# Attention and mixed FFN on one core: the order in which the on-chip tiles are allocated

## The chip, the cores and the metric

One Trainium2 chip, one of its cores. The metric is the device time of one execution in microseconds (us). The kernel before took 3089.31 us, the median of three runs (3080.82, 3089.31 and 3093.53).

## The reference, cut to what matters

```python
x = x + _layernorm(attn(_layernorm(x), w_qkv))      # x: 4 x 2048 tokens x 512
x = x + _layernorm(ffn(_layernorm(x), ...))

# attn: 16 heads of 32, windows of 128 tokens, each window sees the one before and the one after
scores = einsum('bhnqe,bhnke->bhnqk', q * scale, k_ctx)   # k_ctx: 3 windows, 384 keys
out = einsum('bhnqk,bhnke->bhnqe', softmax(scores), v_ctx)

# ffn, for each of the 4 sequences of 2048 tokens its own weights, 8 experts:
g = mean_s(relu(x @ gate_w1.T + gate_b1) @ gate_w2.T + gate_b2)   # 8 numbers per sequence
mW1 = W1 + sum_e g[e] * TW1[e];   mW2 = W2 + sum_e g[e] * TW2[e]   # biases likewise
out = gelu(x @ mW1.T + mb1) @ mW2.T + mb2                          # 2048 hidden units
```

All in float32.

## The kernel before, in words

The program is three functions that run one after the other, each with its own on-chip tiles, which are given back when it ends. In each, every engine has its own list of instructions, and semaphores order them.

`phase_qkv` (A) takes 16 chunks of 512 tokens: layernorm, transposition on TensorE (line 275), and the product with w_qkv (line 280). A float32 product is made as three products of float32r parts (high by high, high by low, low by high). A chunk has 8 groups of 12 matmuls for q and k (w is the stationary operand, the transposed x the moving one) and 4 groups of 12 for v (the other way round: x stationary, w moving). Results go to DRAM.

`phase_attention` (B) has 128 steps, each for two windows of four heads: scores (line 531, k moving) whose maximum VectorE takes (line 666), the transposed scores with the maximum as an added row (line 546, q moving), the exponential on ScalarE (line 637), sums on GpSimd (lines 491 and 501), and the products with v (line 573). The row of maxima is put into the q tile by two small DMAs of SyncE's queue (line 431).

`phase_gate_ffn` begins with the gate (C: residual, layernorm, transposition at line 1131, gate product at lines 1144 to 1146), and goes on to the FFN (E): VectorE mixes eight experts' weights into a base (line 1497) out of a ring that DMAs fill, ScalarE and VectorE split the result into high and low parts (slots 0 and 1 of five in the tiles wa, slots 2 to 4 in wb), and TensorE makes the hidden product (lines 1194 to 1196, weights stationary, y moving) and the output product (lines 1211 to 1213, u stationary, weights moving).

In the profile's rows the operands of a matmul stand as moving, stationary: `e_acc<-e_wa_hi,e_u_hi` has wa moving and u stationary.

What matters for this change is how a tile gets its address. The functions call `sb(name, shape, dtype)` once per tile:

```python
def sb(name, shape, dt):
    return ctx.enter_context(nc.sbuf_tensor("a_" + name, shape, dt))
```

Tiles are laid one behind the other in the order of these calls, in each of the 128 partitions at the same byte, each start rounded up to a multiple of 32 bytes. The first tile of each phase starts at byte 16512, which is a multiple of 128. The large tiles have sizes that are multiples of 1024 bytes, and so all that follow one another have the same offset within 128 bytes; the small ones (4 to 256 bytes) shift what comes behind them.

Of the kernel before, what the change touches and what calls it, by code (L numbers as in the profile page):

```python
# [8 lines left out]
F32 = mybir.dt.float32  # L9
F32R = mybir.dt.float32r  # L10

P = 128
D = 512
# [6 lines left out]
TILES = CH // P  # L20
CHUNKS = TOKENS // CH
EPS = 1e-5
QH = 4
# [4 lines left out]
RING = 9  # L28
# [15 lines left out]
def phase_qkv(nc, x, w_qkv, qk_dram, v_dram):  # L44
# [7 lines left out]
    with ExitStack() as ctx:  # L52
        def sb(name, shape, dt):
            return ctx.enter_context(nc.sbuf_tensor("a_" + name, shape, dt))
# [1 line left out]
        def sem(name):  # L56
            return nc.alloc_semaphore("a_" + name)

        eps = sb("eps", [P, 1], F32)
        stats = sb("stats", [P, TILES, 6], F32)  # L60
        moments = sb("moments", [P, TILES, 2], F32)
        std = sb("std", [P, TILES], F32)
        rstd = sb("rstd", [P, TILES], F32)
        w_in = sb("w_in", [P, KD, 3 * D], F32)
        w_hi = sb("w_hi", [P, KD, 3 * D], F32R)
        w_lo = sb("w_lo", [P, KD, 3 * D], F32R)
        x_in = sb("x_in", [P, 2, TILES, D], F32)
        xn = sb("xn", [P, 2, TILES, D], F32)
        xt_hi = sb("xt_hi", [P, 2, KD, CH], F32R)
        xt_lo = sb("xt_lo", [P, 2, KD, CH], F32R)  # L70
        qk = sb("qk", [P, SLOTS, 2, CH], F32R)
        v = sb("v", [P, 2, TILES, D], F32)
        ident = sb("ident", [P, P], F32)
        turn = [ctx.enter_context(nc.psum_tensor(f"a_turn{i}", [P, CH], F32)) for i in range(2)]
        acc = [ctx.enter_context(nc.psum_tensor(f"a_acc{i}", [P, CH], F32)) for i in range(BANKS)]

# [250 lines left out]
def phase_attention(nc, qk_dram, v_dram, o_dram):  # L327
# [7 lines left out]
    RING = 8  # L335
    BANKS = 3
    UNITS = 2 * QH
    with ExitStack() as ctx:
        def sb(name, shape, dt):
            return ctx.enter_context(nc.sbuf_tensor("b_" + name, shape, dt))  # L340
# [4 lines left out]
        def sem(name):  # L345
            return nc.alloc_semaphore("b_" + name)

        neg_max = sb("neg_max", [P, 2, 2, QH], F32)
        pick = sb("pick", [P, 2 * QH], F32)
        inv_sum = sb("inv_sum", [P, 2, 2 * QH], F32)  # L350
        q_st = sb("q_st", [P, QH, SEQ], F32R)
        k_st = sb("k_st", [P, QH, SEQ], F32R)
        v_sb = sb("v_sb", [P, W, QH * E], F32)
        ones = sb("ones", [P, 2, E], F32)
        probs = sb("probs", [P, RING, QH, 3 * WIN], F32)
        max_rows = sb("max_rows", [2 * QH, 2, WIN], F32R)
        total = sb("total", [P, 2, 2, QH, WIN], F32)
        ident = sb("ident", [P, P], F32)
        out_t = sb("out_t", [P, 2, 3, WIN], F32)
        out = sb("out", [P, 2, 2, QH * E], F32)  # L360
        ps_score = [psum(f"ps_score{i}", [P, 512]) for i in range(BANKS)]
# [392 lines left out]
def phase_gate_ffn(nc, x, gate_w1, gate_b1, gate_w2, gate_b2, o_dram, b1, b2, tb1, tb2, mix_rows,  # L754
# [12 lines left out]
    START = units[0][2]  # L767
# [38 lines left out]
    with ExitStack() as ctx:  # L806
# [3 lines left out]
        def sb(name, shape, dt, stack=ctx):  # L810
            return stack.enter_context(nc.sbuf_tensor("e_" + name, shape, dt))

        def psum(name, shape, stack=ctx):
            return stack.enter_context(nc.psum_tensor("e_" + name, shape, F32))

        w2g = sb("w2g", [P, KD, EXPERTS], F32)
        gate_bias = sb("gate_bias", [EXPERTS, 1], F32)
        gate_sum = sb("gate_sum", [P, KD, CHUNKS], F32)
# [8 lines left out]
        stats = sb("stats", [P, 2, TILES, 6], F32)  # L827
        moments = sb("moments", [P, 2, TILES, 2], F32)
        var = sb("var", [P, 2, TILES], F32)
        rstd = sb("rstd", [P, 2, TILES], F32)  # L830
        shift = sb("shift", [P, 2, 2, TILES], F32)
        c_b1 = sb("c_b1", [P, KD], F32)
        eps = sb("eps", [P, 1], F32)
        ring = sb("ring", [P, 2 * RING, D], F32)
        part = sb("part", [P, 2, 2, D], F32)
        wa_hi = sb("wa_hi", [P, START, 2, D], F32R)
        wa_lo = sb("wa_lo", [P, START, 2, D], F32R)
        x1 = sb("x1", [P, TILES, D], F32)
        bias = sb("bias", [P, D], F32)

        with ExitStack() as gate_mem:
            att = sb("att", [P, 2, TILES, D], F32, gate_mem)
# [13 lines left out]
            ident = sb("ident", [P, P], F32, gate_mem)  # L856
# [740 lines left out]
def attention_and_mixed_ffn(nc, x, w_qkv, gate_w1, gate_b1, gate_w2, gate_b2, b1, b2, tb1, tb2, mix_rows, out):  # L1597

    def scratch(name, shape):
        return nc.dram_tensor(name, shape, F32, kind="Internal").ap()  # L1600

    qk_dram = scratch("qk_scratch", [2, 2, P, QUADS, TOKENS])
    v_dram = scratch("v_scratch", [QUADS, TOKENS, QH * E])
    o_dram = scratch("o_scratch", [QUADS, TOKENS, QH * E])
    x1_dram = scratch("x1_scratch", [TOKENS, D])
    yh_dram = scratch("yh_scratch", [D, TOKENS])
    yl_dram = scratch("yl_scratch", [D, TOKENS])
    mb2_dram = scratch("mb2_scratch", [BATCH, D])
    phase_qkv(nc, x, w_qkv, qk_dram, v_dram)
    phase_attention(nc, qk_dram, v_dram, o_dram)  # L1610
    phase_gate_ffn(nc, x, gate_w1, gate_b1, gate_w2, gate_b2, o_dram, b1, b2, tb1, tb2, mix_rows,
                   x1_dram, yh_dram, yl_dram, mb2_dram, out)
# [39 lines left out]
```

## Time and profile before

| | |
|---|---|
| median of three runs | 3089.31 us |
| the profiled execution | 3080.82 us |
| its span from the first instruction to the last | 3078.9 us |
| TensorE busy | 2904.6 us (94%) |
| VectorE busy | 1984.1 us (64%) |
| ScalarE busy | 1737.0 us (56%) |
| GpSimd busy | 870.8 us (28%) |
| DMA | 697.07 MB, mean 226 GB/s |
| granted TensorE clock, mean share of full speed | 0.974 |

The busy share is an average over four stages: A up to about 580 us, B from there to about 1330, C to about 1600, E to the end. A matmul's recorded duration overlaps the next one's, because they are pipelined: what TensorE needs for one is the distance from its start to the next start.

### The profile page before, as it was taken

The page shows a single profiled execution, that of the slowest core. Times are in us where ns is not written, and L with a number is a line of the kernel's source. Part 1 is how long each engine was busy: PE and PEld are TensorE (multiplying, and loading weights), DVE is VectorE, ACT ScalarE, POOL GpSimd, SP SyncE. Part 2 cuts the span into 40 slices and gives each one's busy share as a digit, 9 for nine tenths or more (in the row PEclk, how much of TensorE's full clock was granted, in tenths as well). Part 3 has the DMA queues.
Part 4 walks back from the last instruction along what each step waited for, and adds up shares of the span by engine and source line. Part 5 has one row for each costly group of instructions (what it writes and reads, how often), then busy time and mean ns, then how long its engine had stood idle before and what let it go on. Part 6 is the DMA issues. An engine that isn't in the chain of part 4 may idle for free.

```text
span 3078.9 us, 55797 instructions
## 1 busy us (share of the span) xinstructions
PE 2904.6 (94%) x20444; PEld 2418.1 (79%) x20444; DVE 1984.1 (64%) x3732; ACT 1737.0 (56%) x3398; POOL 870.8 (28%) x773
## 2 busy tenths in 40 slices
PE   7999999699999999959889999999999999999995
PEld 6888888588888888847777888788887888878884
DVE  4333333278887888857757787776768766796632
ACT  2222222166666667645545666766667666776665
POOL 0000000188887888853310000320006000140004
PEclk9999999799999999979999999999999999999998
DMA  5545554668887887669999777876669655895612
GB/s 194 182 170 177 196 186 164 174 161 193 192 196 182 194 193 193 165 211 361 352 356 332 261 273 252 333 282 235 220 225 388 242 205 206 307 348 204 215 40 96
DMA packets 385299, 697.07 MB, mean 226 GB/s; under 512 B 27912, under 2 KB 160008, under 8 KB 385048
## 3 DMA queue, kind: packets, MB, share of 16 engines
q1 hardware_dynamic: 362912, 635.14, 65.1%
q0 software_dynamic: 9472, 33.56, 2.9%
q10 hardware_dynamic: 12672, 25.17, 2.2%
q8 instruction: 148, 2.42, 0.3%
q14 instruction: 95, 0.78, 0.1%
HBM read 525.45 MB, written 167.78 MB: 225 GB/s over the span
## 4 chain that ended last, share of the span: by engine, by line
PE 42%; DMA 4%; DVE 3%; POOL 2%; ACT 2%; SPq 2%; issue 1%; ACTq 0%; POOLq 0%; DVEq 0%
PE e_hid L1194 7%; PE e_hid L1195 7%; PE e_hid L1196 7%; PE e_acc L1211 7%; PE e_acc L1212 7%; PE e_acc L1213 7%; DMA yl_scratch<-e_yt_lo 3%; POOL e_sums L1114 1%; DVE e_part L1497 1%; DVE e_yt_lo L1447 1%; SPq L976 1%; DVE e_c_stats L1420 1%; DMA e_x<-x_scratch 1%; ACT e_sums L1351 0%; DVE e_c_y L1441 0%
## 5 line engine op out<-in xcount | busy, mean ns | idle before, releaser
L1497 DVE SCALAR_TENSOR_TENSOR e_part<-e_ring,e_g_cols,e_part 128x512 f32<-128x512 f32 x896 | 637.2, 768 | 2.1
L666 DVE TENSOR_REDUCE b_neg_max<-b_ps_score 128x1 f32<-128x384 f32 (+1 forms) x1024 | 491.6, 527 | 73.0 <-PE b_ps_score L531 61.7
L637 ACT ACTIVATE b_probs<-b_ps_keys 128x384 f32<-128x384 f32 (+1 forms) x1024 | 426.9, 478 | 84.4 <-PE b_ps_keys L546 56.9
L1309 ACT ACTIVATE e_u<-e_hid,e_mb 128x512 f32<-128x512 f32 x256 | 177.2, 692 | 436.5 <-PE e_hid L1196 431.1
L1521 DVE TENSOR_TENSOR e_u_lo<-e_u,e_u_hi 128x512 fp32r<-128x512 f32 x256 | 193.0, 754 | 324.2 <-ACT e_u_hi L1313 324.1
L1102 POOL TENSOR_SCALAR e_var<-e_moments 128x4 f32<-128x4 f32 x16 | 8.8, 549 | 1213.2 <-DVE e_moments L1533 1212.3
L531 PE MATMUL b_ps_score<-b_k_st,b_q_st 96*128 96x384 f32 (+1 forms) x1024 | 333.6, 366 | 16.0 <-DMA b_q_st<-qk_scratch 15.7
L491 POOL TENSOR_TENSOR b_total<-b_probs 128x512 f32<-128x512 f32 x256 | 323.9, 1282 | 70.0 <-ACT b_probs L637 70.0
L546 PE MATMUL b_ps_keys<-b_q_st,b_k_st 97*128 97x384 f32 (+1 forms) x1024 | 314.3, 349 | 28.0 <-DMA b_q_st<-b_max_rows 26.7
L237 DVE TENSOR_TENSOR a_qk<-a_acc,a_qk 128x512 fp32r<-128x512 f32 x128 | 88.5, 692 | 345.4 <-ACT a_qk L176 345.4
L501 POOL TENSOR_TENSOR b_total<-b_total,b_probs 128x512 f32<-128x512 f32 x224 | 286.3, 1278 | 64.8 <-ACT b_probs L637 62.3
L1326 ACT ACTIVATE e_sums<-e_acc 128x512 f32<-128x512 f32 x512 | 291.3, 595 | 8.0 <-PE e_acc L1213 5.2
L1337 ACT ACTIVATE e_acc<-e_sums 128x512 f32<-128x512 f32 x448 | 263.9, 614 | 0.0
L1211 PE MATMUL e_acc<-e_wb_hi,e_u_hi 128*128 128x512 f32 x608 | 239.5, 394 | 8.2 <-ACT e_acc L1337 8.1
L1194 PE MATMUL e_hid<-e_y_hi,e_wb_hi 128*128 128x512 f32 x608 | 236.9, 390 | 2.3 <-DVE e_wb_lo L1516 2.3
L1212 PE MATMUL e_acc<-e_wb_lo,e_u_hi 128*128 128x512 f32 x608 | 238.1, 392 | 0.0
L1213 PE MATMUL e_acc<-e_wb_hi,e_u_lo 128*128 128x512 f32 x608 | 238.0, 391 | 0.0
L1195 PE MATMUL e_hid<-e_y_lo,e_wb_hi 128*128 128x512 f32 x608 | 236.8, 389 | 0.0
L1196 PE MATMUL e_hid<-e_y_hi,e_wb_lo 128*128 128x512 f32 x608 | 236.5, 389 | 0.0
L531 PEld LDWEIGHTS b_ps_score<-b_k_st,b_q_st 96*128 96x128 f32 x1024 | 194.9, 193 | 47.2 <-DVE b_neg_max L666 20.6
L176 ACT ACTIVATE a_qk<-a_acc 128x512 fp32r<-128x512 f32 x128 | 76.6, 599 | 268.4 <-PE a_acc L280 268.4
L546 PEld LDWEIGHTS b_ps_keys<-b_q_st,b_k_st 97*128 97x128 f32 x1024 | 191.3, 191 | 41.2 <-DMA b_q_st<-b_max_rows 33.9
(137 smaller groups left out, 6325.3 us busy)
## 6 DMA issues: line engine op xcount, KB each, us to landing
e_ring<-mix_rows SPq DMA_DIRECT2D x558, 512.0 KB, 5.2
qk_scratch<-a_qk SPq DMA_DIRECT2D x128, 512.0 KB, 2.8
b_k_st<-qk_scratch SPq DMA_DIRECT2D x192, 256.0 KB, 4.4
b_q_st<-qk_scratch SPq DMA_DIRECT2D x192, 256.0 KB, 4.2
a_x_in<-x SPq DMA_DIRECT2D x16, 1024.0 KB, 7.2
v_scratch<-a_v SPq DMA_DIRECT2D x64, 256.0 KB, 3.0
b_v_sb<-v_scratch SPq DMA_DIRECT2D x64, 256.0 KB, 4.9
o_scratch<-b_out SPq DMA_DIRECT2D x128, 128.0 KB, 2.9
```

Source lines behind the costliest of these rows:

```text
L491: add = pool.tensor_tensor(total[:, g % 2, i], p[0], p[1], ALU.add)
L531: pe.matmul(ps_score[y % BANKS][:, 0:(hi - lo) * WIN], q_st[0:STACK, h, w * WIN:(w + 1) * WIN], k_st[0:STACK, h, lo * WIN:hi * WIN], start ...
L546: pe.matmul(ps_keys[x % BANKS][:, 0:(hi - lo) * WIN], k_st[0:STACK + 1, h, w * WIN:(w + 1) * WIN], q_st[0:STACK + 1, h, lo * WIN:hi * WIN] ...
L637: act.activation(probs[:, m % RING, h, 0:(hi - lo) * WIN], ps_keys[x % BANKS][:, 0:(hi - lo) * WIN], ACT.Exp, scale=SCALE).then_inc(exp_do ...
L666: dve.tensor_reduce(neg_max[:, g % 2, i, h:h + 1], ps_score[y % BANKS][:, 0:(hi - lo) * WIN], AX_X, ALU.max, negate=True).then_inc(reduced, 1)
L1194: pe.matmul(hid[s % 4][:, :], w_hi(n)[:, 0, cols], y_hi[:, q, k, :], start=(k == 0), stop=False)
L1195: pe.matmul(hid[s % 4][:, :], w_hi(n)[:, 0, cols], y_lo[:, q, k, :], start=False, stop=False)
L1196: mm = pe.matmul(hid[s % 4][:, :], w_lo(n)[:, 0, cols], y_hi[:, q, k, :], start=False, stop=(k == KD - 1))
L1211: pe.matmul(acc[t][:, :], u_hi[:, s % 3, cols], w_hi(n)[:, 1, :], start=False, stop=False, skip_group_check=True)
L1212: pe.matmul(acc[t][:, :], u_hi[:, s % 3, cols], w_lo(n)[:, 1, :], start=False, stop=False, skip_group_check=True)
L1213: pe.matmul(acc[t][:, :], u_lo[:, s % 3, cols], w_hi(n)[:, 1, :], start=False, stop=end, skip_group_check=True).then_inc(used, 1)
L1497: dve.scalar_tensor_tensor(out=part[:, n % 2, half, :], in0=ring[:, slot, :], scalar=g_cols[:, b, e:e + 1], in1=so_far, op0=ALU.mult, op1= ...
```

## The change

The calls of `sb` are put in another order. Nothing else is changed: the instructions of every engine, their order, sizes and semaphores are the same (9716 rows for TensorE, 1505 for VectorE, 1882 for ScalarE, 459 for GpSimd, 634 for SyncE, none moved). Only the addresses in them differ.

```diff
 phase_qkv:
-        eps = sb("eps", [P, 1], F32)
-        stats = sb("stats", [P, TILES, 6], F32)
-        moments = sb("moments", [P, TILES, 2], F32)
-        std = sb("std", [P, TILES], F32)
-        rstd = sb("rstd", [P, TILES], F32)
         w_in = sb("w_in", [P, KD, 3 * D], F32)
         w_hi = sb("w_hi", [P, KD, 3 * D], F32R)
         w_lo = sb("w_lo", [P, KD, 3 * D], F32R)
+        ident = sb("ident", [P, P], F32)
+        eps = sb("eps", [P, 1], F32)
         x_in = sb("x_in", [P, 2, TILES, D], F32)
...
         v = sb("v", [P, 2, TILES, D], F32)
-        ident = sb("ident", [P, P], F32)
+        stats = sb("stats", [P, TILES, 6], F32)
+        moments = sb("moments", [P, TILES, 2], F32)
+        std = sb("std", [P, TILES], F32)
+        rstd = sb("rstd", [P, TILES], F32)
 phase_attention:
-        neg_max = sb("neg_max", [P, 2, 2, QH], F32)
-        pick = sb("pick", [P, 2 * QH], F32)
-        inv_sum = sb("inv_sum", [P, 2, 2 * QH], F32)
         q_st = sb("q_st", [P, QH, SEQ], F32R)
         k_st = sb("k_st", [P, QH, SEQ], F32R)
         v_sb = sb("v_sb", [P, W, QH * E], F32)
         ones = sb("ones", [P, 2, E], F32)
         probs = sb("probs", [P, RING, QH, 3 * WIN], F32)
+        neg_max = sb("neg_max", [P, 2, 2, QH], F32)
         max_rows = sb("max_rows", [2 * QH, 2, WIN], F32R)
         total = sb("total", [P, 2, 2, QH, WIN], F32)
         ident = sb("ident", [P, P], F32)
+        pick = sb("pick", [P, 2 * QH], F32)
+        inv_sum = sb("inv_sum", [P, 2, 2 * QH], F32)
 phase_gate_ffn:
+        ring = sb("ring", [P, 2 * RING, D], F32)
+        part = sb("part", [P, 2, 2, D], F32)
+        wa_hi = sb("wa_hi", [P, START, 2, D], F32R)
+        wa_lo = sb("wa_lo", [P, START, 2, D], F32R)
+        x1 = sb("x1", [P, TILES, D], F32)
+        bias = sb("bias", [P, D], F32)
         w2g = sb("w2g", [P, KD, EXPERTS], F32)
...
         eps = sb("eps", [P, 1], F32)
-        ring = sb("ring", [P, 2 * RING, D], F32)
-        part = sb("part", [P, 2, 2, D], F32)
-        wa_hi = sb("wa_hi", [P, START, 2, D], F32R)
-        wa_lo = sb("wa_lo", [P, START, 2, D], F32R)
-        x1 = sb("x1", [P, TILES, D], F32)
-        bias = sb("bias", [P, D], F32)
```

What the order makes of the addresses, worked out from the sizes and the rounding (the start's remainder by 128 bytes; a remainder of 32 or 96 is 32 above a multiple of 64):

| tiles | start before | by 128 | start after | by 128 |
|---|---|---|---|---|
| A: w_in, w_hi, w_lo | 16736, 41312, 65888 | 96 | 16512, 41088, 65664 | 0 |
| A: x_in, xn, xt_hi, xt_lo, qk, v | 90464 (x_in) | 96 | 90784 (x_in) | 32 |
| A: ident | 188768 | 96 | 90240 | 0 |
| B: q_st, k_st, v_sb, ones, probs | 16672 (q_st) | 32 | 16512 (q_st) | 0 |
| B: max_rows, total, ident | 139808 (max_rows) | 32 | 139712 (max_rows) | 64 |
| B: neg_max | 16512 | 0 | 139648 | 0 |
| B: out_t, out | 149536, 152608 | 32 | the same | 32 |
| E: ring, part, wa_hi, wa_lo, x1, bias | 18016 (ring) | 96 | 16512 (ring) | 0 |
| C: all large tiles (att to cw_lo) | 89696 (att) | 96 | the same | 96 |
| C: ident | 212928 | 64 | the same | 64 |
| E: y_hi, y_lo, sums, wb_hi, wb_lo, u, u_hi, u_lo | 89696 (y_hi) | 96 | the same | 96 |

## Rows read from the trace of the kernel before

**Rows 1.** Busy time by stretch; columns named in the first row.
```profile
core 0: us, PE busy (x) PEld busy (x) DVE busy (x) ACT busy (x) POOL busy (x), PEclk, DMA share, GB/s
60.00:560.00 500.00, 500.00 (x2312) 413.62 (x2311) 178.13 (x347) 134.08 (x244) 0.00 (x0) 1.00 0.53 181
640.00:1300.00 660.00, 646.25 (x9844) 562.55 (x9844) 535.76 (x1308) 455.01 (x1071) 557.64 (x446) 0.99 0.80 191
1360.00:1600.00 240.00, 209.78 (x1020) 172.01 (x1019) 173.21 (x410) 123.26 (x273) 73.04 (x56) 0.95 1.03 350
1600.00:2950.00 1350.00, 1333.31 (x5818) 1096.01 (x5818) 983.90 (x1425) 884.13 (x1551) 140.43 (x160) 0.99 0.74 264
```

**Rows 2.** Timeline of TensorE in A: start us, duration us, instruction.
```profile
99.81 0.39 PE L280 MATMUL a_acc<-a_xt_lo,a_w_hi 128*128 128x512 f32 x1
100.04 0.39 PE L280 MATMUL a_acc<-a_xt_hi,a_w_lo 128*128 128x512 f32 x1
...
101.85 0.39 PE L280 MATMUL a_acc<-a_xt_lo,a_w_hi 128*128 128x512 f32 x1
```

**Rows 3.** The same in B, with 384 and 256 columns.
```profile
701.02 0.34 PE L531 MATMUL b_ps_score<-b_k_st,b_q_st 96*128 96x384 f32 x1
701.19 0.40 PE L546 MATMUL b_ps_keys<-b_q_st,b_k_st 97*128 97x256 f32 x2
701.43 0.73 PE L531 MATMUL b_ps_score<-b_k_st,b_q_st 96*128 96x384 f32 x2
```

**Rows 4.** The same in E, at the full and at the halved clock.
```profile
2400.30 0.39 PE L1211 MATMUL e_acc<-e_wa_hi,e_u_hi 128*128 128x512 f32 x1
...
2402.80 0.39 PE L1213 MATMUL e_acc<-e_wa_hi,e_u_lo 128*128 128x512 f32 x1
...
2001.62 0.63 PE L1212 MATMUL e_acc<-e_wa_lo,e_u_hi 128*128 128x512 f32 x1
...
2003.75 0.63 PE L1211 MATMUL e_acc<-e_wa_hi,e_u_hi 128*128 128x512 f32 x1
```

**Rows 5.** Tile views of the transposes: duration ns, minimum/median/maximum.
```profile
L275 PE MATMUL a_turn<-a_ident,a_xn x256: 270/272/447, 13.2 to 533.3; 128*128 128x128 f32 x128
L591 PE MATMUL b_ps_turn<-b_ident,b_out_t x256: 270/272/421, 630.6 to 1329.2; 128*128 128x128 f32 x128
L1131 PE MATMUL e_turn<-e_ident,e_c_y x256: 272/273/448, 1359.8 to 1585.2; 128*128 128x128 f32 x128
```

**Rows 6.** Groups by line: shapes, count, busy us, mean ns, idle before.
```profile
L280 PE MATMUL a_acc<-a_xt_hi,a_w_hi 128*128 128x512 f32 x512 | 204.7, 400 | 1.4 <-DVE a_xt_lo L231 1.4
L280 PE MATMUL a_acc<-a_w_hi,a_xt_hi 128*128 128x512 f32 x256 | 101.0, 394 | 0.0
L531 PE MATMUL b_ps_score<-b_k_st,b_q_st 96*128 96x384 f32 x896 | 298.4, 374 | 0.2
L1211 PE MATMUL e_acc<-e_wa_hi,e_u_hi 128*128 128x512 f32 x416 | 163.6, 393 | 4.1 <-ACT e_acc L1337 4.0
L1194 PE MATMUL e_hid<-e_y_hi,e_wa_hi 128*128 128x512 f32 x416 | 163.9, 394 | 0.8 <-DVE e_x L1476 0.8
L1497 DVE SCALAR_TENSOR_TENSOR e_part<-e_ring,e_g_cols,e_part 128x512 f32<-128x512 f32 x896 | 637.2, 768 | 2.1
```

**Rows 7.** Who waited for whom: us in total, times, longest.
```profile
PE b_ps_keys L546 <- DMA b_q_st<-b_max_rows: 26.7, 18, 13.2
ACT e_yt_hi L1273 <- DMA yl_scratch<-e_yt_lo: 32.6, 12, 12.7
```

**Rows 8.** VectorE's statistics of A, duration ns minimum/median/maximum.
```profile
L35 DVE BATCH_NORM_STATS2 a_stats<-a_x_in x64: 672/678/695, 6.3 to 502.2; 128x6 f32<-128x512 f32 x64
```

## The prediction

> **What bounds the kernel now.** I read the busy times by stretch first, since the change touches three stages that may have different limits [rows 1]. TensorE is busy for 500.00 of 500 us in A, for 646.25 of 660 in B and for 1333.31 of 1350 in E. The next engine is far behind in A (VectorE, 178.13), at 557.64 of 660 in B (GpSimd) and at 983.90 of 1350 in E (VectorE, 73%). Only in C, 240 us, is another thing in the way: the DMA share is 1.03, and ScalarE waits 32.6 us for a store out of the tile yt_lo [rows 7]. No address of C's large tiles changes. So the question is what an address can do to a matmul, and then what it can do to the others by enough that they reach TensorE.
>
> The timelines give what TensorE needs for one matmul, by the starts. In A nine starts lie between 99.81 and 101.85 us: 2.04/9 = 0.2267 us for 512 columns [rows 2]. In E there are eleven between 2400.30 and 2402.80: 2.50/11 = 0.2273 [rows 4]. The clock is at its upper level there, 2.4 GHz, and 512 columns at one per cycle are 213.3 ns. So every such matmul takes 13.3 ns more than its columns. In B, 384 columns take 0.17 us (701.02 to 701.19) against 160.0 ns, and two matmuls of 256 take 0.24, 0.12 each, against 106.7 [rows 3]: again about 13 ns. At the lower level, 1.2 GHz, five steps from 2001.62 to 2003.75 are 2.13/5 = 0.426 us [rows 4], and 512 columns at 1.2 GHz are 426.7: the excess is gone. I take from this that the 13.3 ns is not spent in TensorE's own cycles (it would be 26.7 at half the clock) but in something beside it, such as the reading of the operands. That is where an address could matter, and it is the one thing in this profile that speaks for a change of time.
>
> **The change part by part.** No instruction is added, removed or moved; each keeps its shape. What changes is the start of some tiles. Before, every large tile is 32 or 96 bytes above a multiple of 128. After, w in A, q, k, v and the probabilities in B, and ring, part and wa in E start at multiples of 128; xt in A, y, u and wb in E stay 32 above a multiple of 64.
>
> Moving operands that become aligned: w for v, three groups of 256 as the row `a_w_hi,a_xt_hi`, 768 matmuls; k and q in B, 896 with 384 columns and 128 with 256 at each of two lines, 2048; wa in E's output product, three groups of 416, 1248 [rows 6]. Together 4064, all in stretches that TensorE fills. Each could change by between -13.3 ns (its whole excess) and some gain of the other sign. The only moving float32 tile of before that starts at a multiple of 64 is C's identity: its transposes take 273 ns in the median, those of A and B, whose identities start at 32 above one, take 272 [rows 5]. So the nearest row gives +1 ns, within the resolution. I take 0: 4064 x 0 = 0 us, with ends of -13.3 x 4064 = -54 us and +1 x 4064 = +4 us. The weight of this row is limited: a transpose of 128 columns takes about twice its columns' time, it reads slower than the float32r matmuls, and so would hide what these cannot.
>
> Stationary operands that become aligned (w for q and k, 1536 matmuls; wa for the hidden product, 1248): weight loads are busy for 413.62 us where the matmuls fill 500 in A, 1096.01 of 1350 in E [rows 1], so they lie beside the matmuls. I take 0; a gain there is hidden, a loss shows only once a load is longer by the 17 to 19% that it has left.
>
> VectorE, ScalarE, GpSimd: the mixing (768 ns in the mean, 896 and 128 times) reads ring and part, both moved [rows 6]. The statistics of A write their six numbers at starts that are 24 bytes apart, so at four offsets, and the 64 durations are 672 to 695 ns with a median of 678 [rows 8]: an offset of the written side is worth at most 23 ns of 678, 3%. Taken for the mixing, 1024 x 0.023 = 24 us, either way, of VectorE's time, against 366 us in which it is idle in E. Nothing of it reaches TensorE: 0 us. The cover would be gone if the mixing took 37% longer.
>
> DMA: the ring loads only have to come before the mixing, which stood idle for 2.1 us in all [rows 6]; a slower load is late only past the ring's nine slots. In B TensorE waits 26.7 us for the row of maxima [rows 7], behind 256 KB loads in SyncE's queue. All loads into q and k change their offset. No row of before separates offset from kind of transfer, so the ends are -27 us (no wait left) and +27 (twice the wait). The row nearest is the wait itself, 18 times in 128 steps; a transfer that takes a few per cent more or less moves it by about 1 us either way, and I take 0.
>
> On this the Trainium skill has a rule against the change: "DMA: Bandwidth & Descriptors", section "How a descriptor splits into AXI transactions", says that a descriptor which does not start at a multiple of 256 bytes is fetched from the boundary below, at a cost in beats of 32 bytes. By it the starts at 128 pay four beats where 32 paid one, three more on 64 for a packet of 2048 bytes, an estimate of about 5% of a load. No row here shows it. It would add little more than 1 us to the sum, if that 5% went to the whole wait.
>
> Sum against the profiled execution's own time: 3080.8 + 0 (moving) + 0 (stationary) + 0 (others) + 0 (DMA) = 3080.8 us. That execution was the fastest of the three shown, 8.5 us below their median of 3089.3. The forecast for the median is therefore 3089 us.
>
> **The rivals.**
> *The excess is the price of an unaligned start (faster).* 13.3 ns are 32 columns, 128 bytes of float32. If the moving tile is read in pieces of 128 bytes at a pace that full clock just needs, 512 columns from an unaligned start touch 17 pieces and not 16: 213.3 x 17/16 = 226.7, the pace measured. 384 columns: 160.0 x 13/12 = 173; 256: 106.7 x 9/8 = 120, and 0.17 and 0.12 are in the rows [rows 3]. At half the clock the reading has time to spare, and the excess is gone, as it is. All fits; but a start-up of fixed length on the reading side fits the same rows equally, and no float32r tile of before is aligned to tell them apart. Gain: 768 + 2048 + 1248 = 4064 x 13.3 = 54 us, all on TensorE where it is the bound (in B GpSimd's 557.64 us leave room for the 27 us there): 3089 - 54 = 3035 us. With pieces of 64 bytes only half would be spared, 27 us: 3062 us.
> The Trainium skill ("SBUF — State Buffer", "Door 1: The DMA port swizzle") gives SBUF's lines as 16 bytes. By that rule a start at a multiple of 32 crosses no line more than one at a multiple of 128, and this rival gives nothing. The rows neither bear this out nor refute it.
>
> *Operands at different offsets get in each other's way (slower).* Before, the moving and the stationary tile of every float32r matmul have the same offset. After, w at 0 meets xt at 32 in all 2304 matmuls of A, and wa at 0 meets y and u at 96 in 2496 of E: 4800 matmuls. The one pair of different offset before, C's identity (64) with c_y (96), has the median that is 1 ns longer [rows 5]. At 1 ns the price is 5 us, 3094, no change. It decides from 3.2 ns on (4800 x 3.2 = 15.4 us, 0.5%). At half the excess, 6.7 ns, it is 32 us: 3121 us. Against it: loads and matmuls at present show no sign of disturbing one another, since all steps are alike.
>
> *A DMA effect in B.* Twice the wait for the row of maxima is 3116 us, none at all 3062. I see nothing for such a size.
>
> **How the numbers follow.** What a measurement can tell from no change is about 0.5%, 15.4 us. No effect beyond that: 0.62, with a range of its own of 3078 to 3101 (the three runs lie at 3081 to 3094, with a few us for the small terms). The price of an unaligned start, in whole or in half, or a shorter wait in B: faster, 0.22. Different offsets, or a longer wait in B: slower, 0.16. The range reaches half-way into both: low 3052 holds the half price of a start (3062) and not the whole (3035), high 3112 holds the small prices of different offsets and not 3121; about 0.1 is left out on either side.
>
> **What would show it.** If I am right, the distance between matmul starts is 0.227 us in A, for wa and wb in E alike, 0.17 and 0.12 in B, and no group of VectorE or ScalarE changes its mean by over 3%. The unaligned start shows at once as a difference within one trace: the steps of wa's output product (aligned) at about 0.214 beside wb's at 0.227. Different offsets show as wa's hidden product slower than wb's. A DMA effect shows in the wait of line 546, and the time in B. I am wrong if TensorE's step changes by over 3 ns in any of these groups, or if the time leaves 3078 to 3101 us with the steps unchanged.

## The result, and the profile after

The changed kernel took 3104.11 us (median of 11 runs, 3095.98 to 3117.18), the kernel before, run beside it, 3080.82 us (11 runs, 3073.57 to 3093.53): a ratio of 1.0069 [1.0049, 1.0089]. It is slower, by 23 us between the medians and by 21 us by the ratio. The forecast was no change (3089 us). The time lies inside the stated range of 3052 to 3112, but the interval of the ratio excludes no change, so the forecast of no change was wrong; the second rival, "operands at different offsets get in each other's way", is what happened.

The profiled execution took 3113.23 us, its span is 3111.3 us. First the busy times by stretch, in the columns of [rows 1]:

```profile
60.00:560.00 500.00, 500.00 (x2264) 404.57 (x2263) 175.34 (x343) 131.82 (x240) 0.00 (x0) 1.00 0.53 176
640.00:1300.00 660.00, 648.26 (x9882) 564.68 (x9875) 535.88 (x1308) 454.86 (x1071) 559.05 (x448) 0.99 0.78 191
1600.00:2950.00 1350.00, 1330.54 (x5756) 1078.67 (x5756) 964.80 (x1397) 867.58 (x1524) 141.03 (x160) 0.99 0.75 264
```

TensorE is as full as before, 500.00 of 500 us in A. But it does 2264 matmuls in them and did 2312: the busy time says nothing, the count says that each takes longer. In B it does a few more (9882 against 9844). The timeline of A, which answers to [rows 2]:

```profile
99.74 0.40 PE L280 MATMUL a_acc<-a_xt_lo,a_w_hi 128*128 128x512 f32 x1
...
102.08 0.40 PE L280 MATMUL a_acc<-a_xt_hi,a_w_lo 128*128 128x512 f32 x1
```

Ten steps lie between these two starts: 2.34/10 = 0.234 us, and were 0.2267. The recorded duration of one has hardly moved (0.39 to 0.40). In E, where wa has moved and wb has not, a stretch that goes from wb to wa and back:

```profile
1805.94 0.39 PE L1194 MATMUL e_hid<-e_y_hi,e_wa_hi 128*128 128x512 f32 x1
...
1808.73 0.40 PE L1211 MATMUL e_acc<-e_wa_hi,e_u_hi 128*128 128x512 f32 x1
...
1811.54 0.40 PE L1194 MATMUL e_hid<-e_y_hi,e_wb_hi 128*128 128x512 f32 x1
...
1814.29 0.39 PE L1211 MATMUL e_acc<-e_wb_hi,e_u_hi 128*128 128x512 f32 x1
...
1817.01 0.39 PE L1194 MATMUL e_hid<-e_y_hi,e_wb_hi 128*128 128x512 f32 x1
```

There are twelve matmuls from each to the next. Hidden product with wa 2.79/12 = 0.2325 us, output product with wa 2.81/12 = 0.2342; then with wb 2.75/12 = 0.2292, and 2.72/12 = 0.2267. So wa costs time as the stationary and as the moving operand, wb does not; the first twelve behind a change from wa are between the two. Over the whole trace, by the same reading of all starts, the mean steps at the full clock are 233.2 ns in A (before 228), 233.1 and 233.3 for wa's two products, 227.8 and 227.1 for wb's (before 226.7 to 226.8 for all four).

At the halved clock, which answers to the second half of [rows 4], the cost is not there: five steps of wa from 1649.08 to 1651.21 are 2.13/5 = 0.426 us, as they were before.

```profile
1649.08 0.63 PE L1196 MATMUL e_hid<-e_y_hi,e_wa_lo 128*128 128x512 f32 x1
...
1651.21 0.58 PE L1195 MATMUL e_hid<-e_y_lo,e_wa_hi 128*128 128x512 f32 x1
```

The other engines have not changed. The mixing of E on VectorE, in the columns of [rows 6]:

```profile
L1497 DVE SCALAR_TENSOR_TENSOR e_part<-e_ring,e_g_cols,e_part 128x512 f32<-128x512 f32 x896 | 636.1, 767 | 2.1
```

The transposes of C, in the columns of [rows 5]:

```profile
L1131 PE MATMUL e_turn<-e_ident,e_c_y x256: 270/273/476, 1370.4 to 1597.9; 128*128 128x128 f32 x128
```

ScalarE's wait for a store of C, in the columns of [rows 7]:

```profile
ACT e_yt_hi L1273 <- DMA yl_scratch<-e_yt_lo: 33.5, 12, 12.2
```

All three read nearly as before: the mean and the median within 1 ns, the wait 33.5 us against 32.6. By the starts of the first and last matmul of each product, of the 32.4 us between the two spans 12.0 are in A (its last product starts at 588.7 against 576.7 us), 16.4 in E (1450.3 against 1433.9) and 5.4 in C, which had 42 us at the halved clock and 26 before; B is 1 us shorter. The halved stretches differ from one execution to the next, so a profile alone overstates the loss here; the timed runs say 23 us.

In the following, "distance" is what the start addresses of the stationary and of the moving tile of a matmul differ by, modulo 256 bytes. A matmul whose distance is not 0 is called unequal. Starts, too, are given as remainders by 256 from here on, where nothing else is said. In A the distance was 0 and became 32 bytes (w at 128, xt at 160); for wa in E it was 0 and became 32 the other way (wa at 128, y and u at 96). The lengths given are of one profiled execution, the ratios of timed runs with their 95% interval.

### The profile page after: what moved, and what is told of

Same layout as the page of the kernel before. It is cut to its first block, busy times and chain, and to the rows that moved or that the text cites. A ratio compares the mean times of both kernels' runs of the same rounds, so it can differ in the third digit from the quotient of the medians.

```text
span 3111.3 us, 55797 instructions
## 1 busy us (share of the span) xinstructions
PE 2938.7 (94%) x20444; PEld 2423.4 (78%) x20444; DVE 1985.4 (64%) x3732; ACT 1737.2 (56%) x3398; POOL 870.9 (28%) x773
## 4 chain that ended last, share of the span: by engine, by line
PE 42%; DMA 4%; DVE 3%; POOL 2%; ACT 2%; SPq 2%; issue 1%; ACTq 0%; POOLq 0%; DVEq 0%
PE e_hid L1194 7%; PE e_hid L1196 7%; PE e_hid L1195 7%; PE e_acc L1211 7%; PE e_acc L1213 7%; PE e_acc L1212 7%; DMA yl_scratch<-e_yt_lo 3%; POOL e_sums L1114 1%; DVE e_part L1497 1%; DVE e_yt_lo L1447 1%; SPq L976 1%; DVE e_c_stats L1420 1%; DMA e_x<-x_scratch 1%; ACT e_sums L1351 0%; DVE e_c_y L1441 0%
```

## The experiments

Filler is a tile nobody uses, put ahead of the tile named. Between these kernels nothing differs in the instructions but the addresses. The lengths of A, B, C and E go from the start of the first matmul to that of the last.

**The change in three parts.** Each kernel has one function of the changed kernel and two of before.

```diff
 a_only:  phase_qkv as changed; phase_attention, phase_gate_ffn as before
 e_only:  phase_gate_ffn as changed; the other two as before
 b_only:  phase_attention as changed; the other two as before
```

> Only phase A has the new order (w at 0, x tiles at 32 by 128 bytes), B and E as before. Theory P (a matmul whose stationary and moving tile lie 32 bytes apart modulo 64 takes 0.233 us instead of 0.227): A's last product starts near 588.7 us instead of 576.7 (12 us later), and the whole is 12 us slower, ratio 1.004; the steps of the product in A are 0.231 to 0.235 us. Theory S (a float32r tile at a multiple of 64 bytes is slow by itself): the same here. Theory N (the difference was scatter in the clock's low stretches): no later end of A.

Measured: 1.0051 [1.0037, 1.0065]; A's last product starts at 589.7 us, steps of 233.2 ns.

> Only the third function has the new order (ring, part, wa at 0; y, u, wb at 96). Theories P and S: A and B as before, the steps of the products with wa 0.231 to 0.235 us, those with wb 0.227 but for a few after a change from wa; about 2496 x 6.5 ns = 16 us slower, ratio 1.005. Theory N: no difference in the steps.

Measured: 1.0052 [1.0035, 1.0070]; steps as in the changed kernel to the tenth of a ns, E 1449.6 us.

> Only phase B has the new order (q, k, v, probabilities at 0, all pairs of a matmul still equal by 64). Theory P: no change, ratio 1.000, B lasts as long as before (716 us from the first to the last score) within 2 us. Theory S: 2048 matmuls with 384 or 256 columns are slower by 4 to 8 ns each, 8 to 16 us. A DMA effect would show in B's length as well.

Measured: 0.9975 [0.9958, 0.9992], so faster, which none of the theories had. The length of B in a single profile does not show it: the profiled execution, the slowest of the ten, has 722.3 us from the first to the last score where 716 +-2 were expected, with 44 us at the halved clock in B (before 35). The parts add up: 0.51 + 0.52 - 0.25 = 0.78%, beside 0.69 [0.49, 0.89] for the whole. The theory by which an aligned start is slow by itself (S) already fails in B, where q and k both moved to a multiple of 128.

**Which property of the address counts.** All four start from the kernel before.

```diff
 all_zero:  +        sb("pad", [P, 8], F32)    # ahead of w_in, and ahead of ring
 apart_32:  +        sb("pad", [P, 8], F32)    # ahead of A's x_in, and ahead of C's and E's shared tiles
 apart_64:  +        sb("pad", [P, 16], F32)   # at the places of apart_32
 apart_256: +        sb("pad", [P, 64], F32)   # at the places of apart_32
```

> The order of before with 32 bytes of filler ahead of w_in in A and ahead of ring in the third function: all large tiles of A, C and E start at multiples of 128 instead of 96 above one. Theory P (only the offset between stationary and moving counts): ratio 1.000, steps 0.227. Theory S (a tile at a multiple of 64 is slow by itself): all 6144 products of E, 2304 of A and 768 of C slower by 6.5 ns, 60 us. The unaligned start as the cause of the 13.3 ns: steps of 0.214, 100 us faster.

Measured: 1.0002 [0.9989, 1.0014], steps of 226.7 ns in E, A 577.4 us. Every float32r tile of A, C and E starts at a multiple of 128 there, and it is not slow (S), nor do the 13.3 ns go (the prediction's first rival). Both theories fall.

> The order of before with 32 bytes of filler between w and the x tiles in A, and between wa and the tiles of C and E: w at 96 and xt at 0; wa at 96, and y, u and wb at 0. The distance of 32 modulo 64 is as in the changed kernel, with the tiles' places exchanged. Theory P: A 12 us longer, the products of wa 0.231 to 0.235 us, in all 23 to 28 us slower, ratio 1.0075 to 1.009. Theory S: wb, y, u (at 0) slow, wb's products included.

Measured: 1.0086 [1.0059, 1.0112]; steps of 233.2 ns in A, 232.8 and 233.6 for wa, 227.5 and 227.0 for wb. The tiles at a multiple of 128 are now xt, y, u and wb, and the same pairs pay.

> The same with 64 bytes of filler: w at 96, xt at 32; wa at 96, and y, u, wb at 32. If what counts is the place within 64 bytes, ratio 1.000 and steps 0.227. If it is the place within 128 bytes or more, A is about 12 us longer and wa's products 0.231 to 0.235 us.

Measured: 1.0071 [1.0048, 1.0095]; 233.4 ns for v's product and 229.4 for that of q and k, 230.4 and 233.3 for wa; A ends at 584.2 us, 7.5 later and not 12. So 64 bytes are not free, as the first of the two readings had it. Here the direction counts, as it does not at 32: with the moving tile 64 bytes above the stationary one (q and k, hidden product) a matmul costs 1.5 and 3.7 ns more, some 30 and 60% of what 32 bytes do; with the moving tile below it (v, output product) it costs as much as at 32. Twelve hidden products with wa take 2.74 us, twelve output products 2.80:

```profile
1804.59 0.39 PE L1196 MATMUL e_hid<-e_y_hi,e_wa_hi 128*128 128x512 f32 x1
...
1807.33 0.39 PE L1213 MATMUL e_acc<-e_wa_hi,e_u_hi 128*128 128x512 f32 x1
...
1810.13 0.39 PE L1196 MATMUL e_hid<-e_y_hi,e_wb_hi 128*128 128x512 f32 x1
```

> The kernel before with 256 bytes of filler between w and the x tiles in A, and between wa and the tiles of C and E. Distances of 32, 64 and 128 bytes between stationary and moving tile have cost time so far, one of 512 has not. If the pattern repeats every 256 bytes: all steps 0.227 us, ratio 1.000. If it repeats every 512: A about 12 us longer, wa's products near 0.233 us, ratio 1.008.

Measured: 1.0003 [0.9986, 1.0020], all steps as before. So a distance of 256 bytes is as good as none. The row of the stretch from 60 to 560 us, in the columns of [rows 1], of apart_32, apart_64 and apart_256:

```profile
60.00:560.00 500.00, 500.00 (x2266) 404.79 (x2265) 175.22 (x343) 131.62 (x240) 0.00 (x0) 1.00 0.53 176
```
```profile
60.00:560.00 500.00, 500.00 (x2286) 409.04 (x2285) 176.05 (x344) 132.44 (x242) 0.00 (x0) 1.00 0.53 178
```
```profile
60.00:560.00 500.00, 500.00 (x2312) 413.65 (x2311) 178.14 (x347) 134.03 (x244) 0.00 (x0) 1.00 0.54 181
```

2266, 2286 and 2312 matmuls in the same 500.00 busy us: the count is the measure.

**One operand alone, and tiles that are no operand.**

```diff
 u_only:    +        sb("pad", [P, 8], F32)    # ahead of u_hi
 xlo_only:  +        sb("pad", [P, 8], F32)    # ahead of xt_lo
 ring_only: +        sb("pad", [P, 8], F32)    # ahead of ring
 ring_only: +        sb("pad2", [P, 24], F32)  # ahead of wa_hi
```

> The kernel before with 32 bytes of filler ahead of u_hi: only u_hi and u_lo are moved (from 96 to 0), the stationary operands of the output product. Theory P: all 3072 matmuls of the output product (lines 1211 to 1213, with wa and with wb) take 0.233 us, the hidden product's stay at 0.227 but for the first ones after an output product; 3072 x 6.5 ns = 20 us slower, ratio 1.0065. A theory by which DMA writes or the mixing at a new offset disturb TensorE gives no change, since neither touches u.

Measured: 1.0066 [1.0044, 1.0088]. Output product 232.8 ns with wa and 232.9 with wb, hidden product 227.7 and 227.8:

```profile
1801.10 0.39 PE L1212 MATMUL e_acc<-e_wb_hi,e_u_hi 128*128 128x512 f32 x1
...
1803.89 0.39 PE L1195 MATMUL e_hid<-e_y_hi,e_wb_hi 128*128 128x512 f32 x1
...
1806.63 0.39 PE L1212 MATMUL e_acc<-e_wa_hi,e_u_hi 128*128 128x512 f32 x1
```

Twelve output matmuls take 2.79 us, twelve hidden ones 2.74, and these are a little longer only because they stand behind the output ones. No DMA touches u, and the weights stayed: the cost goes with the distance between TensorE's two operands.

> The kernel before with 32 bytes of filler ahead of xt_lo in A: of three matmuls of the product in A, the one with xt_lo has unequal offsets, and the two with xt_hi equal ones. If the cost falls on the matmul with unequal operands alone, only a third of the steps grow, and A ends 4 us later (near 581 us). If one unequal matmul spoils the next ones too (in the changed kernel up to 7 steps behind such a one were longer), A ends up to 12 us later (near 589).

Measured on one execution (3097.30 us, so no ratio): A ends at 589.5 us, 12.8 later. One unequal matmul in three costs as much as three in three; all kinds of step are longer (means of 229 to 239 ns). So the price is not one per unequal matmul: it spreads to the ones beside it, as at the changes from wa to wb above.

> The kernel before with filler that puts ring and part of the third function at multiples of 128 instead of 96 above, while wa, wb, y and u keep 96. Theory P (TensorE's two operands): all steps of E 0.227 us and E as long as before (1434 us). If the ring's DMAs or the mixing at their new offset slow TensorE's matmuls, wa's steps are at 0.233 and E is 16 us longer.

Measured on one execution: E 1433.6 us, 226.7 ns in all groups of E but one at 226.8. The row from wa's hidden product:

```profile
1804.21 0.39 PE L1196 MATMUL e_hid<-e_y_hi,e_wa_hi 128*128 128x512 f32 x1
...
1806.48 0.39 PE L1197 MATMUL e_hid<-e_y_lo,e_wa_hi 128*128 128x512 f32 x1
```

Ten steps, 0.227 us each. The ring's DMAs and the mixing have no share. (The whole of that run, 3096.68 us, was longer for B, 750.6 us; B is the same program there as before, and its length in the kernels that leave it alone lies between 736 and 751 us, so the 736.6 us of before are the short end.)

**The changed kernel mended.**

```diff
 mended:     +        sb("pad", [P, 24], F32)    # changed order; ahead of x_in in A
 mended:     +        sb("pad", [P, 8], F32)     # ahead of the tiles of C and E
 mended_512: as mended, with [P, 120] ahead of x_in
```

> The changed order, with 96 bytes of filler ahead of the x tiles in A and 32 bytes ahead of the tiles that C and E share, so that w and xt, and wa, wb, y and u all start at multiples of 128. Theory P: the loss goes, the time is that of the kernel before, ratio 1.000 (0.998 to 1.002), all steps 0.227. Theory S: it gets worse than the changed kernel, ratio 1.010 or more (4800 matmuls plus those of wb and C). The prediction's first rival (13.3 ns for an unaligned start) would show here too: steps of 0.214 and a gain of over 50 us.

Measured: 1.0022 [1.0009, 1.0036]. E is mended (226.7 ns in all groups), A is not (233.2 for q and k, 232.4 for v). All tiles start at multiples of 128 there, but w is at 128 by 256 and xt at 0: a distance of 128 costs like 32. The expectation, of all steps at 227 ns and at most 1.002, had taken 128 bytes for the period.

> The changed order with 480 bytes of filler ahead of A's x tiles (w and xt then differ by a multiple of 512, where the first mended kernel had 128 and A kept steps of 0.233 us) and 32 bytes ahead of the tiles of C and E. Theory P with a distance that must be 0 by 512 (or 256): all steps 0.227 us, A ends near 577 us, and only the gain of the new order in B stays, 6 to 8 us: ratio 0.9975, 3076 us, faster than both kernels. If the remainder of the first mended kernel (ratio 1.0022) had another cause, that stays.

Measured: 0.9979 [0.9963, 0.9995], 3076.75 us; A ends at 576.7 us, all steps as before. With the distances at 0 a small gain stays, of the size of b_only's.

**B's gain, and a faster kernel.** B has no unequal float32r pair in either kernel, but its DMAs write and read tiles at other offsets.

```diff
 all_256:  +        sb("pad", [P, 40], F32)    # ahead of w_in
 all_256:  +        sb("pad", [P, 56], F32)    # ahead of q_st
 all_256:  +        sb("pad", [P, 40], F32)    # ahead of ring
 qk_256:   +        sb("pad", [P, 56], F32)    # ahead of q_st
 qk_256:   +        sb("pad2", [P, 8], F32)    # ahead of v_sb
 rest_256: +        sb("pad", [P, 56], F32)    # ahead of v_sb
```

> The order of before with filler of 160, 224 and 160 bytes ahead of w_in, q_st and ring: every large tile of all phases starts at a multiple of 256 bytes, and every stationary tile has the offset of its moving one. Theory P: all steps 0.227 us. For the DMAs: in A the 2048-byte packets took 91.9 ns in the mean at an offset of 96 and 92.2 at 0 by 256 with the 512-byte ones 29.1 and 27.0; in B 132.5 at 32 and 129 at 128. If a start at a multiple of 256 is the best for a DMA, packets of 2048 bytes in B take at most 129 ns, the waits for the row of maxima shrink below 60 us, C gets shorter by some us, and the ratio is 0.995 to 0.998. If B's gain came from something else, the ratio is 1.000.

Measured: 0.9946 [0.9930, 0.9961], 3068.40 us (3061.42 to 3076.25, 12 runs): faster than both kernels. The queue of the loads and stores in B, from 640 to 1300 us, in the columns packets, MB, share of 16 engines; before, changed, all_256:

```profile
q1 hardware_dynamic: 116120, 124.24, 78.7%
```
```profile
q1 hardware_dynamic: 115798, 124.34, 76.9%
```
```profile
q1 hardware_dynamic: 116856, 124.25, 74.9%
```

The same bytes take less of the engines' time. By size, in the same stretch: the 2048-byte packets (loads into q and k) took 132.4 ns in the mean with the tiles at 32, 129.1 at 128 and 127.7 at 0; the 512-byte ones 35.7, 35.0 and 32.8. Other kernels bear it out: in the ten whose q and k lie at 32 and whose B is otherwise unchanged the 2048-byte packets took 132.2 to 134.1 ns, in the four with them at 128 it was 128.4 to 129.3. TensorE's and its loader's waits for the row of maxima went from 60.6 us to 55.0 and 42.3; in the ten kernels with B unchanged they are 60.6 to 79.7, and b_only has 65.0.

> The kernel before with filler in B only, so that q_st and k_st start at multiples of 256 bytes, and all other tiles of B keep their offset of 32. If the packets of the q and k loads (2048 bytes into those tiles) are what made B shorter: their mean is 127 to 129 ns instead of 132.5, the 512-byte packets stay at 35.4, the wait for the row of maxima goes below 60 us, and the ratio is 0.9955 to 0.998. If it was another tile, 1.000.

Measured: 0.9990 [0.9979, 1.0000]; 2048-byte packets 127.5 ns, 512-byte ones 35.2, waits 53.1 us. The packets do as expected, the time less.

> The other half: q_st and k_st stay at 32, and v_sb, probs, max_rows, total, ident, out_t and out start at multiples of 256. If the q and k loads alone count, ratio 1.000. The stores from out and the loads into v are of 512-byte packets: if their start counts, the mean goes from 35.4 to about 33 ns, and the ratio is below 0.999; both halves add up to about the 0.9946 of all_256 (in which A and C changed too).

Measured: 0.9993 [0.9982, 1.0004]; 133.4 and 33.5 ns, waits 55.5 us. Each half shortens its own packets, and neither alone can be told from no change with certainty; together they make 0.17%, where b_only had 0.25 [0.08, 0.42] and all_256 0.54%. That the packets' time depends on the tile's offset is shown; that it is all of the gain is not. What in all_256 gave the rest stays open: its profiled execution has B at 731.7 us (before 736.6, the other kernels with that B up to 750.6), E at 1430.4 (1433.9, with 3 us less at the halved clock) and A the same.

## Why the prediction was wrong, by its steps

- *TensorE is the bound in A, B and E*: right. The loss in A and E is the growth of TensorE's step times the number of steps.
- *The 13.3 ns are not spent in TensorE's own cycles, and an address could matter there*: the excess itself has nothing to do with the address. It is the same with both operands at 96, 128 or 0 (before, all_zero, all_256): 226.7 ns in E. But the reasoning from the halved clock holds for the new cost: it too is gone there.
- *Moving operands that become aligned, taken at 0*: this is the step that failed, in what it asked. It looked for a price of one tile's start, between -13.3 and +1 ns for 4064 matmuls. There is none; there is a price of the distance between two tiles, and the term belongs on the 4800 matmuls that the second rival counted, which the sum left out. That rival was sized at +1 ns by the transposes [rows 5], though the text said itself that these read slower and would hide what a float32r matmul cannot. They do hide it: the change took A's transposes, too, from a distance of 0 to one of 32 bytes, and the mean distance between their starts went from 108.4 to 108.7 ns, while the product's went up by 5. Measured: 5.2 ns in A (233.2 less 228.0) x 2304 = 12.0 us, 6.5 ns for wa x 2496 = 16.2, and 1.1 and 0.4 ns for wb (a mean of all, those behind wa being the longer ones) x 1824 each = 2.7 us, so 31 us at the full clock. E is 16.4 us longer by the profile and not 18.9, since it had 17 us at the halved clock and 31 before, which takes off about 4, and pauses of 2 us more.
- *Stationary operands, taken at 0 because loads lie beside matmuls*: wrong for the same reason. The loads' own time did not change (188 ns), and the loss came all the same; the loads' durations do not show it and the matmuls' hardly. So the sign named there, a load longer by what it has left, was the wrong one; that room is also misread, since 500 against 413.62 and 1350 against 1096.01 let a load grow by 21 and 23% and not by 17 to 19. u_only moved stationary tiles alone and cost 0.66%.
- *Other engines 0*: right; the mixing 767 ns in the mean against 768.
- *DMA 0, with ends of +-27 us*: the sign was open, the size small: with B's new order alone the kernel is 0.25% or 8 us faster. That the DMAs are all of it is not shown. The Trainium skill's rule ("DMA: Bandwidth & Descriptors", "How a descriptor splits into AXI transactions") would have made the q and k loads longer at 128 than at 32; they were shorter by 3.3 ns. In A it agrees: the 512-byte stores out of v took 27.0 ns from a start at a multiple of 256 (all_256, mended), 28.9 to 29.1 from a start at 96, and 29.8 to 30.1 from starts at 128 and 160.
- *The rival priced at 6.7 ns, 32 us, 3121 us, with 0.16*: right in mechanism, count and size. What spoke against it in the text, "all steps are alike", was no evidence: before, the distance was 0 in every float32r matmul. Nor was C's identity the one unequal pair of before: in B the identity (32) meets neg_max, which starts at 128, and pick (192) meets out_t (32), both float32 and short. The time it gives, 3121 us, starts from 3089; the measured 3104 is 3081 + 31 - 8.
- *The forecast's base*: 3089 was the median of three runs; over 11 the kernel before is at 3081. The range was held by luck in part: with 3081 as its base its upper end would have been 3104, the measured time. The narrower range for no effect, 3078 to 3101, was left, and so was the text's own limit of 3 ns for a step. Nor was 0.5% the least that can be told from no change: with 11 runs each the interval is +-0.2%.

## What to carry to other kernels

In a kernel whose bound is TensorE with float32r matmuls of 512 columns, look at the start addresses of each matmul's stationary and moving tile: here differences of 32, 64 and 128 bytes cost 1.5 to 7 ns of 227, those of 0, 256 and 512 nothing (96, 160, 192 and 224 were not run, nor other column counts), and 32 bytes of small tiles ahead of a large one were enough to cause it. Check it with the number of matmuls in a fixed stretch or the distance between starts, since busy time and durations hide it. Start every large tile at a multiple of 256: that makes all distances 0, and the kernel here that does so (all_256) is 0.54% faster than before, where the distances were 0 already. Shorter DMA packets go with that gain; how much of it they make is open.

An absence of a sign in a trace where the suspected condition never occurs is no argument against it: price such a rival by what it would cost, and ask what else in the layout has been equal so far.

## What the runs showed of the hardware that was not expected

- A float32r matmul's step depends on the distance between its stationary and its moving tile: at the full clock it grows by 0 at a distance of 0, 256 or 512 bytes, by 5 to 7 ns a matmul at 32 and 128, and at 64 by 6 to 7 with the moving tile below the stationary one and by 1.5 to 4 with it above; at the halved clock, seen at a distance of 32, it does not grow (0.426 us). That the reading of the two tiles gets in each other's way fits this, and is not shown; in which part of the chip it arises, no run shows.
- One unequal matmul in three is as dear as three in three (589.5 against 588.7 us for A's end), and equal ones behind an unequal one are longer as well.
- DMA packets into tiles at 0, 128 and 32 by 256 bytes took 127.7, 129.1 and 132.4 ns in B.
